# Experts' second layer with w2 stationary, and softmax sums applied to the heads' output

## The reference

```python
x = _L0_conv_ref(x, ...)          # a recurrence over 16 rows (ConvLSTM), 96 channels, batch 16, 16x16
t = _to_tokens(x)                 # (16, 256, 96)
t = t + attn(_ln_t(t))            # 6 heads of 16, causal over 256 tokens, softmax, then @ Wp + bp
t = t + ffn(_ln_t(t))
# ffn: 4 experts, 96 -> 384 -> 96, the best two of four weighted
probs = softmax(x @ gate_w + gate_b); mask = top 2
masked = probs * mask; masked = masked / (sum(masked) + 1e-9)
h = gelu(einsum('bsd,edh->ebsh', x, w1) + b1)
y = einsum('ebsh,ehd->ebsd', h, w2) + b2
out = einsum('bse,ebsd->bsd', masked, y)
```

## Time and profile before

| | |
|---|---|
| three runs | 469.58, 470.88, 472.49 us; median 470.88 |
| profiled execution, span | 469.8 us |
| recurrence | about the first 80 us |
| a middle block | 44.2 us |
| PE, DVE, ACT, POOL busy in the span | 91%, 57%, 56%, 31% |

### The profile page before, as it was taken

One profiled execution on the slowest core, in us unless ns is written; L12 is line 12 of the kernel. 1 busy time (PEld: TensorE's weight loads), 2 busy tenths in 40 slices (PEclk: granted clock), 3 DMA queues, 4 the chain that ended last, 5 costly groups with the idle time before them and its releaser, 6 DMA issues.

```text
span 469.8 us, 10623 instructions
## 1 busy us (share of the span) xinstructions
PE 429.3 (91%) x3112; PEld 344.1 (73%) x3112; DVE 269.8 (57%) x954; ACT 263.7 (56%) x740; POOL 146.5 (31%) x309
## 2 busy tenths in 40 slices
PE   6999995449779999999999999999999999999897
PEld 6989994325558767877787787778767877787676
DVE  3888887445523853585277527743763586267424
ACT  2444453236557556664866485568556664866370
POOL 5000000235521542254236215531543254235200
PEclk9999998557979999999999999999999999999999
DMA  8500000031021002100210121012002100210000
GB/s 201 130 0 0 0 0 0 17 71 32 3 57 29 19 0 59 44 17 14 66 38 0 38 51 28 0 46 52 19 0 54 46 0 4 76 22 3 7 11 17
DMA packets 14392, 14.93 MB, mean 32 GB/s; under 512 B 5426, under 2 KB 11412, under 8 KB 14372
## 3 DMA queue, kind: packets, MB, share of 16 engines
q1 hardware_dynamic: 14180, 14.30, 12.1%
q0 software_dynamic: 192, 0.39, 0.3%
HBM read 3.86 MB, written 1.57 MB: 12 GB/s over the span
## 4 chain that ended last, share of the span: by engine, by line
PE 73%; DVE 12%; ACT 5%; issue 5%; SPq 2%; DMA 1%; POOL 1%; DVEq 1%; ACTq 0%; POOLq 0%
PE F L1018 18%; PE T L976 9%; PE A L997 8%; PE F L1034 4%; PE F L1038 4%; PE S L960 4%; PE F L1035 4%; PE S L962 3%; PE F L1014 3%; PE S L965 2%; DVE c L629 2%; DVE ig L627 2%; ACT tc_sb L471 2%; DVE pt_sb L457 1%; PE M L939 1%
## 5 line engine op out<-in xcount | busy, mean ns | idle before, releaser
L406 POOL TENSOR_SCALAR p_sb<-p_sb,rden 128x128 f32<-128x128 f32 (+1 forms) x192 | 79.8, 431 | 135.0 <-DVE rden L710 132.8
L1018 PE MATMUL F<-w_sb,hid 128*128 128x96 f32 x768 | 101.0, 276 | 0.0
L1018 PEld LDWEIGHTS F<-w_sb,hid 128*128 128x128 f32 x768 | 93.4, 192 | 6.0 <-issue 6.0
L518 ACT ACTIVATE p_sb<-S,nmax 128x128 f32<-128x128 f32 (+1 forms) x192 | 78.9, 425 | 17.1 <-DVE nmax L704 17.0
L704 DVE TENSOR_REDUCE nmax<-S 128x2 f32<-128x512 f32 (+1 forms) x80 | 50.7, 634 | 52.7 <-PE S L965 52.3
L457 ACT COPY pt_sb<-T 128x512 f32<-128x512 f32 (+1 forms) x48 | 26.4, 550 | 68.7 <-PE T L976 68.7
L564 ACT ACTIVATE hid<-F,b_sb 128x512 f32<-128x512 f32 x72 | 49.3, 686 | 9.6 <-PE F L1038 9.0
L997 PE MATMUL A<-pt_sb,v_cur 128*32 128x128 f32 x576 | 44.2, 284 | 8.5 <-ACT pt_sb L457 4.5
L976 PE MATMUL T<-id_sb,p_sb 128*128 128x128 f32 x288 | 49.2, 290 | 1.5 <-POOL p_sb L406 1.4
L960 PE MATMUL S<-k_bd,q_st 96*128 96x384 f32 (+2 forms) x96 | 39.3, 416 | 6.5 <-DMA k_bd<-k_cur 6.4
L976 PEld LDWEIGHTS T<-id_sb,p_sb 128*128 128x128 f32 x288 | 30.9, 143 | 16.3 <-issue 13.9
(11 more groups left out here) (140 smaller groups left out, 781.8 us busy)
## 6 DMA issues: line engine op xcount, KB each, us to landing
k_bd<-k_cur SPq DMA_DIRECT2D x96, 32.0 KB, 2.0
q_st<-q_cur SPq DMA_DIRECT2D x28, 96.0 KB, 2.2
k_bd<-k_cur SPq DMA_DIRECT2D x96, 16.0 KB, 1.8
t_st<-t_cm SPq DMA_DIRECT2D x7, 192.0 KB, 2.4
out_y<-y_sb SPq DMA_DIRECT2D x7, 192.0 KB, 1.9
x_pad<-in_x SPq DMA_DIRECT2D x2, 612.0 KB, 8.6
w_sb<-in_w SPq DMA_DIRECT2D x1, 576.0 KB
hid<-in_w SPq DMA_DIRECT2D x1, 576.0 KB, 6.9
```

The lines of the kernel that those rows point to most:

```text
L406: last = nc.gpsimd.tensor_scalar(p, p, rden[:, u % 3, i:i + 1], 1.0, ALU.mult, ALU.mult)
L518: last = nc.scalar.activation(p_sb[:, u % 3, i * nk:(i + 1) * nk], S[u % 2][:, i * nk:(i + 1) * nk], ACT.Exp, bias=nmax[:, u % 3, i:i + 1] ...
L1018: last = mm(dst[:, e * C:(e + 1) * C], hid[:, c, s * TT:(s + 1) * TT], w2_sb[:, c], start=False, stop=(c == NCH - 1), skip_group_check=True)
```

## The change

The second layer is turned round. For each chunk, w2 (128x96) is stationary and all 512 tokens of `hid` move, so there are 12 matmuls of 512 columns, one bank per expert, and no bias matmul. The result has channels on partitions. So the gates must lie along the columns: `turn_gates` (PE) transposes them, `take_gates` (ACT) copies them, and `spread_gates` (SP) stores them to DRAM and loads them back to all 96 partitions as `gates_cm`. `combine` (DVE) now works per expert on 96x512: (y + b2) times the gate, and a sum. `turn_y` (PE) transposes the sum back, and `finish` (DVE) adds `t1p`.

The softmax scaling no longer touches the probabilities. ACT's row sums go to `den` per tile, DVE inverts them once per tile, POOL spreads the six numbers of a token over 96 columns (`spread`), PE turns them (`turn_sums`, bank M), ACT copies them (`take_spread`), and DVE multiplies the heads' output with them (`heads_out`, which was ACT's copy).

The order is new: `FILL` and `TAIL` count chunks now, `EARLY_T0` goes from 1 to 4, `EARLY_XT` from 4 to 9, and the output projection stands ahead of the values of its slot. The middle of the diff:

```diff
-FILL = [16, 3, 3, 2, 3, 3, 2, 2, 2, 0]
-TAIL = SPB * NCH - sum(FILL)
-TAIL_EARLY = min(TAIL, 9)
+FILL = [4, 0, 1, 0, 1, 0, 1, 0, 1, 0]
+TAIL = NCH - sum(FILL)
+TAIL_FIRST, TAIL_EARLY = 1, 3
-EARLY_T0, EARLY_XT = 1, 4
+EARLY_T0, EARLY_XT = 4, 9
+COMBINE_AT = (4, 6)
...
+            def spread_gates(n, first=False):
+                wait_alone(sp, gate_copied, n + 1)
+                sp.dma_start(gate_hbm.rearrange("e s t -> s e t"), gate_t[:]).then_inc(gate_out, 16)
+                wait_alone(sp, gate_out, 16 * n + 16)
+                if not first:
+                    wait_alone(sp, gated, E * n)
+                sp.dma_start(gates_cm[:], gate_hbm.rearrange("e s t -> (e s t)").unsqueeze(0).to_broadcast((C, E * BT))
+                             ).then_inc(gate_in, 16)
...
                 if more:
                     wait_alone(sp, tt_ready, n + 2)
                     stage(n + 2)
+                if not first:
+                    spread_gates(n - 1, first=not store)
...
-            def combine(n, s, first):
-                dve.wait_ge(y_ready, 4 * n + s + 1)
...
+            def combine(n, e, first):
+                dve.wait_ge(y_ready, E * n + e + 1)
+                if e == 0:
+                    dve.wait_ge(gate_in, 16 * n + 16)
...
+                dst = y_part[:, e % 2] if e else y_cm[:]
+                V.scalar_tensor_tensor(dst, Y[e][0:C, :], b2_sb[:, e:e + 1], gates_cm[:, e], ALU.add, ALU.mult
+                                       ).then_inc(gated, 1)
+                if e:
...
+                    V.tensor_tensor(y_cm[:], y_cm[:], dst, ALU.add).then_inc(summed, 1)
...
-                    if not first and j:
-                        for s, c in out_parts(j - 1):
-                            if c == NCH - 1:
-                                combine(n - 1, s, second)
+                    if not first and j in COMBINE_AT:
+                        combine(n - 1, COMBINE_AT.index(j), second)
...
+            def turn_sums(n, s, last=False):
+                if s == 1 and not last:
+                    pe.wait_ge(t0_done, n + 2)
+                elif s == SPB - 1 and not last:
+                    pe.wait_ge(x1lo_done, n + 2)
+                elif s:
+                    pe.wait_ge(t1_done, 4 * n + s)
+                else:
+                    pe.wait_ge(v_done, n + 1)
...
+                pe.wait_ge(rden_spread, 4 * n + s + 1)
+                mm(M[0:C, 0:TT], rden_c[:].rearrange("p r d -> p (r d)"), id_sb[:], start=True, stop=True
+                   ).then_inc(spread_ready, 1)
...
-                    last = mm(dst[:, e * C:(e + 1) * C], hid[:, c, s * TT:(s + 1) * TT], w2_sb[:, c],
-                              start=False, stop=(c == NCH - 1), skip_group_check=True)
+                    last = mm(dst[0:C, :], w2_sb[:, c], hid[:, c, :], start=(c % CPE == 0), stop=(c % CPE == CPE - 1))
...
+                        for s in range(SPB - 1):
+                            if j == TILE_END[s]:
+                                turn_sums(n, s, last)
+                            if j == TILE_END[s] + 1:
+                                project_out(n, s)
+                        if j == EARLY_T0 and not last:
+                            pe.wait_ge(t1_done, 4 * n + 1)
+                            tokens_first(n + 1)
...
+                        values(n, j - 1, first)
```

More of the change, by code:

```diff
@@ L267, in out_parts @@
         def out_parts(slot):
-            return [divmod(i, NCH) for i in range(sum(FILL[:slot]), sum(FILL[:slot + 1]))]
+            return range(sum(FILL[:slot]), sum(FILL[:slot + 1]))
         def wait_alone(eng, semaphore, value):
@@ L364, in _ @@
             store_y(NBLK - 2)
[L365 to L368, removed]
+            spread_gates(NBLK - 1)
+            store_y(NBLK - 1)
+            sp.wait_ge(y_out, 16 * NBLK)
         @block.gpsimd
@@ L397, in residual, with spread @@
                                         ALU.add).then_inc(tb_done, 1)
[L399 to L407, removed]
+            def spread(n, s, first=False):
+                wait_alone(pool, rden_done, 4 * n + s + 1)
+                if s or not first:
+                    wait_alone(pool, spread_ready, 4 * n + s)
+                nc.gpsimd.tensor_copy(rden_c[:], rden[:, s % 2].unsqueeze(2).to_broadcast((128, HEADS, HS))
+                                      ).then_inc(rden_spread, 1)
             def x1_whole(n):
@@ L514, in exps @@
                     act.wait_ge(pt_ready, NU * n + u - 2)
-                _, t, _ = UNITS[u]
+                a, t, h0 = UNITS[u]
+                s = 2 * a + t
+                if h0 == 0 and (s > 1 or not first):
+                    act.wait_ge(rden_done, 4 * n + s - 1)
                 nk = TT * (t + 1)
@@ L538, in body @@
                         if j == TILE_END[s]:
-                            heads_out(n, s, first)
+                            take_spread(n, s, first)
+                    if j == EARLY_XT and not last:
+                        take_x1(n + 1)
                     if j in PT_ON_ACT:
@@ L545, in body @@
                         take_t0(n + 1)
-                    if j == EARLY_XT and not last:
-                        take_x1(n + 1)
-                heads_out(n, SPB - 1, first)
+                    if j == 1 and not first:
+                        take_gates(n - 1)
+                take_spread(n, SPB - 1, first)
                 if not last:
@@ L812, in body @@
                             normalize2(n, s)
+                heads_out(n, SPB - 1, first)
                 attn_residual(n, SPB - 1)
+                if not first:
+                    combine(n - 1, 2, second)
                 if not last:
@@ L821, in body @@
                 if not first:
-                    for s in range(sum(FILL[:-1]) // NCH, SPB):
-                        combine(n - 1, s, second)
+                    for e in range(3, E):
+                        combine(n - 1, e, second)
                 route(n, 0)
+                if not first:
+                    finish(n - 1, second)
                 if not last:
@@ L842, in _ @@
             route(NBLK - 1, 2)
-            for s in range(SPB):
-                combine(NBLK - 1, s, False)
+            for e in range(E):
+                combine(NBLK - 1, e, False)
+            finish(NBLK - 1, False)
         @block.tensor
@@ L1078, in body @@
                     project_q(n + 1)
+                turn_sums(n, SPB - 1, last)
                 values(n, NU - 1, first)
@@ L1099, in body @@
                 expert_hidden(n, range(3, 6), first)
+                if not first:
+                    turn_y(n - 1)
                 wait_alone(pe, route_copied, n + 1)
```

193 lines of the change are left out of this document (109 added, 84 removed).

## The result

| | before | changed |
|---|---|---|
| median (4 runs each) | 471.15 us | 543.1 us (541.2 to 544.3) |
| span of the profiled execution | 469.8 | 542.5 |
| mean granted clock | 0.959 | 0.897 |
| a middle block (five of them) | 44.2 | 54.75 to 55.5 |
| the sixth block, the last block | 44.2, 41.4 | 48.5, 41.6 |

The changed kernel is slower: ratio 1.152 (95% interval 1.148 to 1.156). The forecast was 529, with a range of 475 to 556.

A forecast was written before the change was run, and what follows sets the result against it. PE's instruction stream (busy 91% of the span) was taken to bound the kernel. 469.8 + 41 (five blocks) + 3.4 (sixth) + 1.5 (last) + 1 (first) + 4.8 (end) + 7.5 (clock) = 529.0; forecast 529 us, range 475 to 556.

The forecast's parts named there:

- The mechanism: Slot 4 of five blocks: gates' transfers queue behind t_st, DVE idles 6 to 8 us before combining; case's chance 0.64.
- Rival 1: Gates' stall in slots 4 to 6 mostly covered by PE's lead, 1 to 5 us a block left: 475 to 500; chance 0.17.
- rival 3: Gain and loss cancel, the stall being 1 us a block: within 1% of before; chance 0.06.
- Rival 2: At slot 4's combining the gates are no wait, PE's stream sets the time: 455 to 465 us; chance 0.13.
- rival 4: Gates' load slow at 10.8 us, five blocks and the end 6.3 longer each: 567; chance inside the forecast case's 0.64.
- PE waits for ACT's t0, the heads, the residual: Three new PE waits in a block, slots 4 onward: 1.7, 3.3 and 2.7 us, 7.7 in all.
- record of 512 columns: Second layer on PE: F32 record takes 0.435 us, two records a matmul, 10.4 us a block instead of 12.9.
- A block: Each of the five blocks whose gates' transfers stand behind t_st: +8.2 us, 41 in all, plus 1.5 each for the clock.
- The first block: No second layer before it: +1 us, the wait for t0 less POOL's part.
- The end: Program's end: gates need transpose, copy, store 2.0 and load 4.5 before the first combining: +4.8 us.
- My clock term: PE's granted clock falls to 0.50 once in each of five blocks: 1.5 us each, 7.5 in all.
- The sixth block and the last: Sixth block: no t_st load ahead, gates in at about 15, stall 2 us: +3.4; last block: +1.5.

The follow-up runs named there:

- Experiment 1: Changed kernel with the gates' store and load put ahead of the load of t_st on SP's queue, nothing else; 511.1 us, ratio 1.086.
- experiment 2: Changed kernel with the first two combining steps moved from slots 4 and 6 to slots 7 and 8, nothing else; 512.4 us.
- experiments 1 to 4: Changed kernel with gates ahead of t_st (511.1 us), combining in slots 7 and 8 (512.4), gates ahead and combining in 6 and 8 (509.7), constant gates without transfers (502.7).
- experiment 9: Changed kernel with old softmax, slots and last-block second layer, whole 512-column pieces, gates ahead of tokens, combining in slots 7, 8 and after keys; 464.8 us, ratio 0.986.
- gates_first: Same run as Experiment 1: changed kernel with the gates' transfers ahead of the load of t_st on SP's queue; 511.1 us, ratio 1.086.
- experiment 4: Changed kernel with gates a constant 0.25, their store, load and SP's waits left out, transpose and ACT's copy kept; 502.7 us.
- combine_late: Same run as experiment 2: changed kernel with the first two combining steps in slots 7 and 8 instead of 4 and 6; 512.4 us.
- old_softmax_late_combining: As old_softmax, but combining in slots 7 and 8 instead of 6 and 8 and the third one behind the keys; 498.0 us, ratio 1.059.
- old_softmax: Changed kernel with gates ahead of t_st, combining in slots 6 and 8, and the earlier kernel's softmax scaling on POOL; 495.9 us, ratio 1.053.

## Why the prediction was right, and where its sizes were off

**The mechanism** was the forecast's: gates' transfers behind `t_st`, DVE idle in slot 4 ahead of the combining, released by the gates' DMA, in five blocks; the sixth shorter; the clock at 0.50 once a block. Experiment 1 takes it away by the queue order alone and gives back 32 us, experiment 2 by DVE's order alone and gives back 31. Rival 1 (mostly covered) and rival 3 fell with the time. Rival 2 (the gates are no wait, PE's stream sets the time, 455 to 465) had a wrong price: with the wait for the gates gone or short the changed kernel takes 503 to 512 (experiments 1 to 4). Its 455 to 465 come only with the old softmax, slots and end: 464.8 in experiment 9. Of rival 4, the text says that it lies inside the forecast's upper end; its 567 is outside the range of 475 to 556. And the sum of 529.0 with 1.1 around it is 530.1, not 529. Neither matters for the outcome.

**Step by step**, from the block's start at 318.09:

| | predicted | measured |
|---|---|---|
| slot 4's scores | 11.0 | 10.8 |
| `t_st` issued | 13.0 | 12.9 |
| the gates' load issued | 15.8 | 15.8 |
| its landing | 4.5, at 20.3 | 5.1, at 20.9 |
| DVE stands | 6.9 | 8.0 |
| PE waits for ACT's t0, the heads, the residual | 1.7, 3.3, 2.7 | 1.6, 2.5, 1.6 |
| query projection | 33.0 | 35.1 |
| record of 512 columns | 0.435 | 0.429 ((5.31 - 0.59) / 11) |

**The terms that were mis-sized.**
- *A block*: +8.2 and 1.5 for the clock, 9.7 in all; measured 10.9 (five blocks, mean 55.1). The total is close because two errors go against each other. PE's busy time at a clock of 1.00 can be read in gates_first, where two blocks are as long and differ in the clock:

```profile
201.29:249.49 48.20, 44.18 (x258) 28.30 (x257) 25.91 (x76) 28.34 (x82) 8.39 (x17) 0.96 0.18 46
346.95:395.14 48.19, 42.59 (x257) 27.51 (x257) 25.90 (x76) 28.41 (x82) 8.39 (x17) 1.00 0.18 45
```

  So PE's work in a block is 42.6 us, 0.6 less than before, where I took 1.2 less. The five blocks have 46.6 us of busy time in the mean, so 4.0 come from the clock, where I took 1.5; the sixth has 44.20 at 0.96. And PE's idle time grew by 7.5 us, from 1.0 to 8.5, where my 8.2 holds 9.4 of waits. That makes 7.5 - 0.6 + 4.0 = 10.9 against 9.4 - 1.2 + 1.5 = 9.7. How much of the clock's 4.0 us makes the block longer is not shown: in the two rows above 1.6 us of it cost nothing. I had sized the low stretch by the one in the first block, 6.6 us with 5.84 busy. The stretches here are longer:

```profile
336.00:341.00 5.00, 2.46 (x7) 0.74 (x5) 1.92 (x6) 0.30 (x1) 0.00 (x0) 0.50 0.36 90
341.00:345.00 4.00, 3.16 (x14) 1.79 (x14) 3.86 (x15) 2.12 (x9) 1.83 (x3) 0.50 0.00 0
345.00:350.00 5.00, 4.27 (x22) 2.59 (x24) 3.14 (x11) 1.28 (x5) 0.78 (x2) 0.57 0.00 0
```

  Part of it is hidden, as I said: the waits at 340.92 and 345.73 came out shorter than predicted because PE came to them late.
- *The first block*: +1 predicted, +5.5 measured (the second layer's first matmul starts at 152.35, before at 146.80). It has two new waits for the turned sums, 1.50 and 2.33 us; I had counted only the first, because there are no gates there. Behind the second one the clock fell once more than before, which had 1.00 from 118.0 to 128.5:

```profile
124.50:130.30 5.80, 5.39 (x34) 3.88 (x31) 2.30 (x9) 2.19 (x6) 1.56 (x4) 0.50 0.01 1
```

- *The end*: +4.8 predicted, +8.3 measured. The last three matmuls, which wait for the first combinings, stood behind a pause of 5.7 us and so ran at the lower level (granted clock 0.54):

```profile
523.79 2.79 PE L1099 MATMUL F<-hid,w_sb 128*96 128x512 f32 x6 [0.44 <-ACT gate_t L568]
532.26 5.16 PE L1099 MATMUL F<-hid,w_sb 128*96 128x512 f32 x6 [5.68 <-DVE y_part L823]
```

  That is 2.4 us, and the load was 0.6 slower than I took. My clock term counted the five blocks and neither end of the program.
- *The sixth block and the last*: +4.3 and +0.2, for 3.4 and 1.5.

By terms: 54.4 for the five blocks where I had 48.5, then 4.3, 0.2, 5.5 and 8.3 against 3.4, 1.5, 1 and 4.8. They add to 72.7, which is what the spans differ by; I had 59.2.

**What the prediction read too simply.** The sum gave nearly all of a block's loss to the gates. With the gates in time (experiment 1) the five blocks are 6.4 us shorter, of 10.9; without any gates' way (experiment 4) a block is still 4 to 5.5 us too long. Its two causes are the turned sums, whose 0.9 us of PE work (my estimate) cost 1.7 a block, and the new order, above all the slots of the next block's turns with the projections' place, which I treated only as a delay for SP: with the old order 22 us go, and which part of it counts was not tried. The prediction had these waits in its walk (t0 and the residual), but as consequences of the late gates; gates_first shows the same waits with the gates in time.

**The two rules.** The four passes that the Trainium skill (FP8 and Floating Point Precision, TensorE Precision Notes) gives for true FP32 agree with 0.429 us for a record of 512 columns: two records a matmul, each at about two cycles a column; that the change is therefore a loss does not hold, since PE's busy time in a block falls by 1.9 us (experiment 9), where I had 2.5 less 0.5 for the turns of gates and y, 2.0. The fit in the Trainium skill (DMA: Bandwidth & Descriptors, Anatomy of one DMA) gives an estimate of 3.8 us for the load of 768 KB; every one of the eight took 4.8 to 5.3. The section gives that fit for transfers issued by GpSimd, and this load goes by SP's queue, so the difference is no proof against it. One reading of mine was rounded: 0.233 us for 512 F32R columns is 9% more than one column a cycle at 2.4 GHz (0.213).

## What to carry to other kernels

A wait has a place in a queue: ask what else stands behind it on that engine, and move either the transfer ahead or the reader back; each alone gave back 31 to 32 us here. Work that is hidden is worth almost nothing to remove (POOL's scaling: 2.7 us of 470, all in the first block), and what replaces it should not touch the engine that bounds the kernel: the turned sums cost 13.8 us. And ask of a coarse order what it makes others wait for: the late turns and the projections' place cost 22 us. A form that pays where other work lies beside it can lose at the end of the program, where nothing does: use the old form for the last block.

## What the hardware showed that I had not expected

- After a PE pause of 5.7 us at the end, the next matmuls ran wholly at the lower clock level: six records of 512 columns in 5.16 us for 2.79. In combine_late the same six took 4.37 us after 5.6 us, so there they got the higher level back on the way. After much shorter pauses the clock fell in some blocks and not in others: in old_softmax_late_combining a wait of 1.36 to 1.40 us is followed by transposes of 1.08 us in four blocks and, after the same 1.40, of 0.64 us in two; in old_softmax a wait of 1.03 us is followed by 0.64 us in four blocks and by 0.78 and 0.98 in two. So at these lengths the clock's answer is not decided by the pause alone, and what decides it stays open.
- A low clock need not cost time: in gates_first a block with a granted clock of 0.96 and 44.18 us of PE busy time is as long (48.20) as one at 1.00 with 42.59 (48.19).
- A load of 768 KB that reads the same 8 KB for 96 partitions took 4.8 to 5.3 us in all eight loads (median 5.1), once for each block.
